# Leaving the unused columns of 64 rows out of a causal attention kernel's relative-position write and skewed read

## The reference, cut to what matters

```python
def _skew(QEr):
    B, H, R, C = QEr.shape
    padded = jnp.pad(QEr, ((0, 0), (0, 0), (0, 0), (1, 0)))
    return padded.reshape(B, H, C + 1, R)[:, :, 1:, :]
...
QEr = jnp.einsum('bhsd,ld->bhsl', q, Er_s)
Srel = _skew(QEr)
QK = jnp.einsum('bhsd,bhtd->bhst', q, k)
attn = (QK + Srel) / math.sqrt(dh)
attn = jnp.where(causal[None, None], attn, -jnp.inf)
out = jnp.einsum('bhst,bhtd->bhsd', jax.nn.softmax(attn, axis=-1), v)
```

## Time and profile before

| | us |
|---|---|
| median of 3 runs | 1283.88 (1282.5 to 1286.7) |
| the profiled execution: its own time | 1286.1 |
| its span, first to last instruction | 1284.6 |
| causal attention within it | about 81 to 397 |

### The profile page before, as it was taken

How to read it: one execution, slowest core, us unless ns; L and a number is a source line. 1 busy time by engine, 2 the same in 40 slices (tenths; PEclk the granted TensorE clock), 3 DMA queues, 4 the chain that set the end, 5 groups by cost and what they waited for, 6 DMA issues and landing times. The chain is left out here.

```text
span 1284.6 us, 22764 instructions
## 1 busy us (share of the span) xinstructions
PE 1011.8 (79%) x6434; PEld 632.7 (49%) x6435; DVE 696.2 (54%) x2140; ACT 647.5 (50%) x1346; POOL 223.0 (17%) x531
## 2 busy tenths in 40 slices
PE   5746778788783746999999993355899999997487
PEld 3414444455452425999999992121333333334344
DVE  4735778888887621010101101475766666684597
ACT  2435777777772212333232331143677777763787
POOL 0000000000000360111111112701222222240232
PEclk9865999999996877999999997576999999998799
DMA  7478889999998657665666641345211111110001
GB/s 247 149 258 307 321 329 337 344 341 339 337 324 329 237 180 240 189 214 185 208 196 195 208 147 50 103 157 155 63 47 46 47 44 48 44 38 9 1 29 39
DMA packets 93319, 227.41 MB, mean 177 GB/s; under 512 B 9686, under 2 KB 51766, under 8 KB 87254
## 3 DMA queue, kind: packets, MB, share of 16 engines
q1 hardware_dynamic: 86454, 208.20, 46.5%
q0 software_dynamic: 6816, 18.62, 5.3%
HBM read 143.07 MB, written 83.62 MB: 176 GB/s over the span
## 5 line engine op out<-in xcount | busy, mean ns | idle before, releaser
L684 DVE CUSTOM_DVE_ANT_0 unused<-mpsS,mask_bias 128x512 bf16<-128x512 f32 x256 | 172.0, 691 | 82.8 <-PE mpsS L617 82.7
L711 ACT ACTIVATE mPT<-mpsB 128x512 f32<-128x512 f32 x256 | 152.6, 597 | 80.0 <-PE mpsB L624 73.7
L1358 ACT ACTIVATE hT<-ph,w 128x128 f32<-128x128 f32 x312 | 89.0, 368 | 198.0 <-PE ph L1332 198.0
L464 PE MATMUL psT<-ident,scores 128*128 128x128 f32 x640 | 108.6, 286 | 58.0 <-ACT scores L557 56.1
L1377 DVE TENSOR_TENSOR ys<-py,b 128x256 f32<-128x256 f32 x39 | 16.6, 425 | 249.3 <-PE py L1342 249.3
L512 DVE CUSTOM_DVE_ANT_0 scores<-psS,bias 128x512 f32<-128x512 f32 (+3 forms) x256 | 119.7, 487 | 53.1 <-DMA bias<-rel 45.1
L1332 PE MATMUL ph<-xT,w 128*128 128x128 f32 x1248 | 146.8, 276 | 0.0
L552 ACT COPY stage<-psE 128x512 f32<-128x512 f32 (+1 forms) x192 | 97.5, 510 | 97.6 <-DMA rel<-stage 70.8
L1332 PEld LDWEIGHTS ph<-xT,w 128*128 128x128 f32 x1248 | 143.7, 193 | 0.1
L1342 PE MATMUL py<-w,hT 128*128 x624 | 141.2, 379 | 0.7 <-DVE ys L1377 0.7
L557 ACT ACTIVATE scores<-scores,nm 128x128 f32<-128x128 f32 (+3 forms) x256 | 136.8, 566 | 5.2 <-DVE nm L525 5.2
(11 more groups left out here) (247 smaller groups left out, 1482.5 us busy)
## 6 DMA issues: line engine op xcount, KB each, us to landing
rel<-stage SPq DMA_DIRECT2D x64, 640.0 KB, 6.7
bias<-rel SPq DMA_DIRECT2D x64, 640.0 KB, 7.2
w<-in_w1p SPq DMA_DIRECT2D x39, 1028.0 KB
qk<-packed SPq DMA_DIRECT2D x64, 192.0 KB
mqk<-packed SPq DMA_DIRECT2D x64, 192.0 KB
w<-in_w2p SPq DMA_DIRECT2D x8, 1024.0 KB
slots_in<-zero_row SPq DMA_DIRECT2D x1, 4992.0 KB, 18.2
xs<-slots_in SPq DMA_DIRECT2D x39, 128.0 KB
```

Source lines behind the costliest of these rows:

```text
L464: tr = nc.tensor.transpose(psT[bank][:, to:to + P], scores[slot][:, at:at + P], ident[:, :])
L684: nc.vector.tensor_tensor_reduce(out=unused[:, i, :], in0=psS[i % 2][:, :], in1=mask_bias[:, i, :], scale=1.0, scalar=-3.0e38, op0=ALU.add ...
L711: nc.scalar.activation(PT[r][:, j, :], psB[j % 2][:, :], ACT.Exp, scale=1.0 / 4).then_inc(s_exp, 1)
```

## The change

The blocks are laid out anew in the 1280-column row (`UNIT_AT`): block 1 at column 0, block 2 at 256, block 0 at 640, block 3 at 768. So the row falls into two segments of 640 columns (`SEG`), each with two blocks. Rows 64 to 127 of a block are written and read whole, as before. For rows 0 to 63, which the skew shifts by 64 columns or more, the write leaves out the first 64 columns of each segment, and the read the last 64. Each of these rows thus becomes two runs of 576 columns (2304 bytes) in place of one of 1280 (5120 bytes). The borders inside a segment are not trimmed.

The write and the read of a head become two transfers each, on the same queue and the same semaphore; everything that waited for 16 now waits for 32. So that the cells left out hold something finite, `opening` fills those of `rel` with zeros (four small transfers), and DVE clears the first 64 partitions of the four `bias` buffers at the start of `causal_attention`. SP waits for that before the first read.

```diff
+UNIT_AT = [768, 256, 0]
+TRIM = P // 2
+SEG = 640
...
 READ, in SP's step:
-                            sp.wait_ge(s_wr[slot], 16 * (turn + 1))
+                            sp.wait_ge(s_wr[slot], 32 * (turn + 1))
...
-                            skewed = bass.AP(rel[slot].ap().tensor, P - 1, [[REL_W - 1, P], [1, REL_W]])
-                            sp.dma_start(bias[slot][:, :], skewed).then_inc(s_rd[slot], 16)
+                            rel_t = rel[slot].ap().tensor
+                            if isinstance(n, int) and n == -READ:
+                                sp.wait_ge(s_blank_bias, RING)
+                            sp.dma_start(bias[slot][TRIM:P, :], bass.AP(rel_t, P - 1 + TRIM * (REL_W - 1), [[REL_W - 1, P - TRIM], [1, REL_W]])
+                                         ).then_inc(s_rd[slot], 16)
+                            sp.dma_start(bias[slot][0:TRIM, :].rearrange("p (g c) -> p g c", c=SEG)[:, :, 0:SEG - TRIM],
+                                         bass.AP(rel_t, P - 1, [[REL_W - 1, TRIM], [SEG, 2], [1, SEG - TRIM]])).then_inc(s_rd[slot], 16)
 REL, in SP's step:
-                            wait(sp, s_rd[slot], 16 * turn)
-                            sp.dma_start(rel[slot][:, :], stage[slot % 2][:, :]).then_inc(s_wr[slot], 16)
+                            wait(sp, s_rd[slot], 32 * turn)
+                            sp.dma_start(rel[slot][TRIM:P, :], stage[slot % 2][TRIM:P, :]).then_inc(s_wr[slot], 16)
+                            sp.dma_start(bass.AP(rel[slot].ap().tensor, TRIM, [[REL_W, TRIM], [SEG, 2], [1, SEG - TRIM]]),
+                                         stage[slot % 2][0:TRIM, 0:REL_W].rearrange("p (g c) -> p g c", c=SEG)[:, :, TRIM:SEG]).then_inc(s_wr[slot], 16)
 DVE, at the start of causal_attention:
+                    for r in range(RING):
+                        nc.vector.memset(bias[r][0:TRIM, :], 0.0).then_inc(s_blank_bias, 1)
 SP, in opening:
+                        sp.wait_ge(s_blank, 1)
+                        for r in range(RING):
+                            sp.dma_start(bass.AP(rel[r].ap().tensor, 0, [[REL_W, TRIM], [SEG, 2], [1, TRIM]]),
+                                         blank[:, :, :]).then_inc(s_blank, 16)
```

More of the change, by code:

```diff
@@ L82, in build @@
         s_const = sem("s_const")
+        s_blank = sem("s_blank")
         s_ctx = [sem(f"s_ctx{i}") for i in range(2)]
@@ L384, in causal_attention @@
             WU = [u[-1][1] + u[-1][2] for u in units]
-            place = {i: (512 * u + off, w) for u, unit in enumerate(units) for i, off, w in unit}
+            place = {i: (UNIT_AT[u] + off, w) for u, unit in enumerate(units) for i, off, w in unit}
             key_place = {j: (512 * u + off, w) for u, unit in enumerate(CAUSAL_KEYS) for j, off, w in unit}
@@ L403, in causal_attention @@
                 s_rd = [sem(f"s_rd{r}") for r in range(RING)]
+                s_blank_bias = sem("s_blank_bias")
                 names = ("emm", "eev", "smm", "soft", "nm", "exp", "tmm", "tev", "seen", "seensp")
@@ L502, in step @@
                             m, slot, turn = soft
-                            dve.wait_ge(s_rd[slot], 16 * (turn + 1))
+                            dve.wait_ge(s_rd[slot], 32 * (turn + 1))
                             wait(dve, s_tmm, NU * (m - RING + 1))
@@ L510, in step @@
                                 for i, off, w in unit:
-                                    at = 512 * u + off
+                                    at = UNIT_AT[u] + off
                                     ttr = nc.vector.tensor_tensor_reduce(
@@ L543, in step @@
                         if early and (not isinstance(n, int) or early[0] >= 2):
-                            act.wait_ge(s_wr[(r + REL - 2) % RING], 16 * (it * (ROUND // RING) + (r + REL - 2) // RING + 1))
+                            act.wait_ge(s_wr[(r + REL - 2) % RING], 32 * (it * (ROUND // RING) + (r + REL - 2) // RING + 1))
                         if soft:
@@ L551, in step @@
                                 act.wait_ge(s_emm, NU * m + i + 1)
-                                nc.scalar.copy(stage[slot % 2][:, 512 * i:512 * i + WU[i]],
+                                nc.scalar.copy(stage[slot % 2][:, UNIT_AT[i]:UNIT_AT[i] + WU[i]],
                                                psE[(NU * slot + i) % 2][:, 0:WU[i]]).then_inc(s_eev, 1)
@@ L734, in opening @@
                     above = sb(c1, "above", [P, P])
+                    blank = sb(c1, "blank", [TRIM, 2, TRIM])
                     s_er, s_above, s_cc, s_es, s_pick = (sem(f"s_{n}") for n in ("er", "above", "cc", "es", "pick"))
@@ L764, in _ @@
                         sp.wait_ge(s_pick, 16 * PIECES)
+                        sp.wait_ge(s_blank, 16 * RING + 1)
                         k.stored(sp)
@@ L801, in _ @@
                         nc.vector.memset(zero_row[:, :], 0.0).then_inc(s_cc, 1)
+                        nc.vector.memset(blank[:, :, :], 0.0).then_inc(s_blank, 1)
                         nc.vector.memset(V[:, :, :, DH:VW], 1.0).then_inc(s_cc, 1)
```

## The result

The changed kernel is slower: 1329.43 us (median of 4 runs, 1322.9 to 1335.24) against 1284.16 us of the kernel before beside it, a ratio of 1.0349 with a 95% interval of 1.0298 to 1.0401. The forecast was 1279.6 us, with a range up to 1286.0. The profiled execution took 1330.19 us (span 1328.7), 44.1 more than the profiled one of before.

A forecast was written before the change was run, and what follows sets the result against it. The prediction took the six DMA engines that carry `qk` loads for the bound. Savings of 4.6 us in bytes and packets and 0.3 us more at the stage's start made -4.3 us, from 1283.88 to 1279.6 us, range 1275.5 to 1286.

The forecast's parts named there:

- Do the new transfers use all engines?: Causal stage's writes and reads: claimed that transfers of 64 rows run on 16 engines, like those of 128.
- bytes and packets: Causal stage's writes and reads: shorter rows minus added landing packets save 86 ns a head, 4.6 us over 54 heads.
- The six engines as the bound: Causal stage: the six DMA engines carrying `qk` loads work 4.35 of a head's 4.44 us and set the pace.
- SP: Causal stage: two more issues a head raise SP's issuing from 1.43 to 2.7 us, covered by its waits; no cost.
- Second halves: Second transfer of each pair: issued while the first half moves; no gap, or 0.2 us where the queue is empty.
- Blanks in `opening`: Four zero-filling transfers in `opening`: SP 1.7 to 3.8 us late there but catches up; cost nothing, 3.8 us without cover.
- The start of the stage: First write and read of the causal stage, queue nearly empty: gaps add 0.3 us, range 0 to 1.
- Cost per transfer: Rival, causal stage: a 30 ns gap at each transfer eats most of the gain; 1282.8 us, chance 0.25.
- Dear packets: Rival, trimmed rows: packets of odd size cost more; 1287.3 us if in the write alone, 1295 in both; chance 0.08.
- Bytes only: Rival, trimmed rows: packets cost nothing, only bytes count; 8.0 us less, 1276.2 us; chance 0.08.
- Latency loop: Rival, causal stage: write landing time is latency, so a later second write adds 0.42 us a head; 1307 us, chance 0.06.
- Fixed cost in series: Rival, causal stage: 1.6 us fixed per transfer, paid twice more each head, adds 173 us; 1457 us, chance 0.01.

The follow-up runs named there:

- Run 1: The changed kernel with all four half transfers on SBUF partitions 32 to 95: 1282.17 us, ratio 0.9973 to the kernel before.
- run 3: The kernel before with each whole write and read cut at partition 64 into two, nothing trimmed: 1332.5 us, ratio 1.0383.
- 5: The changed kernel's write in halves, with the read whole but cut at column 640 into two transfers: 1291.33 us, ratio 1.0042 to the kernel before.
- 6: The changed kernel's read in halves, with the write whole but cut at column 640 into two transfers: 1328.68 us, ratio 1.0305 to the kernel before.
- 11: Write in halves, read cut by columns, with the `qk` load on sixteen engines: 1290.13 us, ratio 1.0025 to the kernel before.
- 12: Read in halves, write cut by columns, with the `qk` load on sixteen engines: 1278.99 us, ratio 0.9921 to the kernel before.
- run 7: The kernel before with `packed` laid out so that `qk` loads use sixteen engines: 1274.9 us, ratio 0.9911.
- run 8: The changed kernel with `packed` laid out so that `qk` loads use sixteen engines: 1294.72 us, ratio 1.0040 to the kernel before.
- 13 to 15: Read of partitions 0 to 63 first: in the changed kernel 1322.86 us, with only the read in halves 1320.93, in the changed kernel with `qk` on sixteen engines 1295.14.
- run 4: The kernel before with each write and read cut at column 640 into two transfers of all 128 partitions: 1288.94 us, ratio 1.0032.
- run 2: The changed kernel's cells cut into one 128-row transfer and one small transfer of rows 64 to 127, each direction: 1285.21 us, ratio 0.9998 to before.

## Why the prediction was wrong

**The step that failed is "Do the new transfers use all engines?".** It asked how many engines a transfer of 64 rows runs on, answered sixteen, and took the price of a packet from rows of whole transfers: 190.5 ns for a row of 5 KB. All engines do run (share 1.07), but on one half of the partitions their packets take longer: in the first transfer twice as long, the same 5 KB row at 218 GB/s in place of 430, and over a write in two halves 238 in place of 382. The count of engines was right and did not settle the rate. (On eight engines a transfer would also have brought each engine 4 rows more, not the 8 that the step names.) Run 1 shows it by giving the same transfers other partitions, and run 3 by cutting the kernel before in halves and nothing else.

**How large it is.** A head moves 2 x (320 + 288) KB, or 1.245 MB, through half transfers. At the 238 GB/s of the first write's two halves that would be an estimated 5.2 us, if the reads go as the writes do and nothing else takes time. The head measured 5.13, with the `qk` load in it. The same measure gave 4.50 before, so the forecast was 4.50 - 0.09 = 4.41; the 0.72 more, times 63, are 45 us. With the later start of the stage they are the loss and the missing gain together. The size thus fits half transfers at the rate of the first write, but it does not come as a fixed price for each: with `qk` on six engines the read's halves cost nearly all of it, with `qk` on sixteen engines the write's more than the read's. **Why that is so stays open.** Tried were the direction (5, 6, 11, 12), the spread of `qk` (7, 8) and the order of the read's halves (13 to 15); none gives a rule. Not tried was the order of the write's halves.

**The bytes and packets** (-4.6 us) were right in kind: run 1 keeps them, loses the half rate and gains 4.7 us against its chip (0.0027 x 1286.83 = 3.5 by the ratio; the interval goes from 0.4 to 6.4). By its writes a head took 4.39 us where before's took 4.50, the forecast difference being 0.09, though this profiled execution was the fastest of ten. The sum itself has a slip: it multiplies by 54, the heads of the stretch read, where the stage has 64. With 64 the -86 ns a head make -5.5 us, and the forecast 1278.7.

**The six engines as the bound** fit what run 7 shows: it relieves them and gains 0.9%, some two thirds of it between the first write and the last. It also shortens SP's issue of the load from 0.78 to 0.34 us, but SP was waiting 2.3 us a head. What comes next, by the waits PE and ACT waiting for each other at 4.37 us a head, was not seen. "DVE, 3.75 us a head" is a busy time, and says nothing of a loop through several engines.

**SP** was forecast at 2.7 us of issuing a head and measured 2.98 in the head shown, covered by its waits for ACT as said. **Second halves** without a gap: as said, since the share is 0.94 and over. **Clearing `bias`**: forecast 5.1 us on DVE, done at 86.5; measured 4 x 1.125 = 4.5, done at 88.1 (later since the stage began later), hidden from the first read at 94.1. **Blanks in `opening`**: their issues took 0.6 us each and the first write came 1.0 us later, but with `qk` on six engines the first write came between 86.9 and 88.8 in the kernels that hold them and between 87.6 and 88.5 in those that do not, so this is no cost that can be told from none. **The start of the stage** was put at +0.3 and measured +3.2 beyond that 1.0 us. The first read, which waits for the first write, already comes at 94.1 against 91.02: here each half transfer is waited for with nothing else in the queue.

**The rivals.** Cost per transfer: run 4 has it, 2 us by the medians and 4 by the ratio (0.3%), not 47. Dear packets: run 2 rules them out. Bytes only: its gain of 7.7 us lies just outside run 1's interval, 0.4 to 6.4, while my sum lies within it. Latency loop: it forecast 1307 from later issues; the issues came later, but run 1, whose second write is issued 0.6 us after its first, gains where this rival would lose. Fixed cost in series: ruled out by run 4. (The Trainium skill's 2.0 us, which the forecast names there, is fitted in that section to transfers that GpSimd issues; SP issued these.) None of them had a place for the rate of a half transfer. The forecast's own signs did show the fault: a head at 5.13, well above the 4.44 that it had named as wrong.

## What to carry to other kernels

Before a transfer is cut, look at which partitions each part lies on, and not only at its bytes, its runs and its number of engines: here cutting at partition 64 cost 3.8% and cutting the same bytes at a column 0.3%. A rise in the busy share of the DMA engines with fewer bytes a second means slower packets, and GB/s over share in a stretch where one transfer is alone helps to find which. Where a transfer uses only some of the engines, as `qk` did, spreading it evenly can be worth more than trimming bytes (0.9% against 0.3%), until the next loop takes over.

## What the runs showed of the hardware that was not expected

- A transfer of 64 partitions moved 218 GB/s on partitions 64 to 127 and 410 on partitions 32 to 95, both with all engines busy and packets of 5 KB. The Trainium skill (SBUF — State Buffer, section "Door 1: The DMA port swizzle") gives the map of partitions to ports by which 32 to 95 reach all sixteen; the two rates agree. The second half of a write went at 325 to 337 GB/s on eight of them, with all engines busy, which that map does not explain.
- A write in two halves at the start of the stage moved 238 GB/s over both, against 382 for a whole one; in the steady stretch a head with four half transfers took 5.13 us, against 4.50.
- With the `qk` load on sixteen engines half transfers cost 20 us (run 8 over run 7), with it on six 45 (changed over before), at nearly the same pace of the engines (306 and 296 GB/s).
- Issuing a transfer took SP 0.32 us for a whole `rel` write, 0.48 to 0.60 for each of the half transfers.
